# Node rows stored early, expert results added to them in DRAM by chained scatters

## The reference

```python
x = x + _L0_gnn_ref(_layernorm(x), src, dst, ...)      # six diffusion steps over 100 k edges
x = x + _L0_ffn_ref(_layernorm(x)[None], ...)[0]       # below

logits = einsum('bsd,de->bse', xn, Wr) + br
top_vals, top_idx = jax.lax.top_k(logits, 2)
w = jax.nn.softmax(top_vals, axis=-1)                  # two weights per node
for e in range(8):
    h = gelu(einsum(xn, W1[e]) + b1[e])
    y = y + (einsum(h, W2[e]) + b2[e]) * w_full[..., e, None]
```

## Time and profile before

| | us |
|---|---|
| median of 3 runs (range) | 1309.59 (1305.15 to 1309.78) |
| profiled execution, its own time | 1307.75 |
| its span, first to last instruction | 1305.6 |
| busy: PE, DVE, ACT, POOL | 1182.4, 726.9, 401.8, 201.5 |
| expert tiles: first scatter to last scatter | 1066.32 to 1275.06 |
| from the last scatter to the end of the span | 30.5 |

### The profile page before, as it was taken

One profiled execution on the slowest core, in us unless ns is written; L12 is line 12 of the kernel. 1 busy time (PEld: TensorE's weight loads), 2 busy tenths in 40 slices (PEclk: granted clock), 3 DMA queues, 4 the chain that ended last, 5 costly groups with the idle time before them and its releaser, 6 DMA issues.

```text
span 1305.6 us, 27942 instructions
## 1 busy us (share of the span) xinstructions
PE 1182.4 (91%) x7835; PEld 824.2 (63%) x7835; DVE 726.9 (56%) x1533; ACT 401.8 (31%) x785; POOL 201.5 (15%) x245
## 2 busy tenths in 40 slices
PE   5798999999999999999999999978998578898990
PEld 3586776665666666666666666645665367777770
DVE  7889999973444344432543444325556757644555
ACT  2675656550000000000221111101211154464553
POOL 2000000000111111111000000000111154455530
PEclk8998999999999999999999999998999789999995
DMA  6110011014443344323441233112333121122257
GB/s 158 45 50 25 25 37 31 28 37 121 100 99 83 61 109 103 88 55 77 130 129 40 85 108 104 57 29 60 114 112 111 52 86 58 62 71 72 75 151 208
DMA packets 76319, 106.02 MB, mean 81 GB/s; under 512 B 12929, under 2 KB 61880, under 8 KB 76108
## 3 DMA queue, kind: packets, MB, share of 16 engines
q1 hardware_dynamic: 62500, 72.44, 18.8%
q0 software_dynamic: 11376, 25.55, 8.7%
q10 hardware_dynamic: 2356, 6.93, 2.2%
HBM read 76.99 MB, written 37.49 MB: 88 GB/s over the span
## 4 chain that ended last, share of the span: by engine, by line
PE 70%; DVE 12%; issue 9%; DMA 3%; DVEq 2%; ACT 2%; POOL 1%; ACTq 1%; another core or an unknown queue 0%; SPq 0%; POOLq 0%
PE ps L1921 41%; PE ps L1899 7%; PE ps L2084 6%; PE ps L2070 6%; PE ps L1867 4%; DVE v_b L1165 3%; PE ps L1972 2%; POOL v_a L769 1%; PE ps L1835 1%; DMA h_ring<-h_dram 1%; PE ps L2056 1%; DMA adj<-y_dram 1%; PE ps L1846 1%; DVE adj L1072 1%; PE ps L2005 0%
## 5 line engine op out<-in xcount | busy, mean ns | idle before, releaser
L1921 PE MATMUL ps<-v_a,adj 125*125 125x512 f16 x1375 | 297.3, 379 | 0.0
L1921 PE MATMUL ps<-v_b,adj 125*125 125x512 f16 x1250 | 270.2, 379 | 1.8 <-DVE v_b L1190 1.8
L1921 PEld LDWEIGHTS ps<-v_a,adj 125*125 (+1 forms) x1375 | 187.6, 136 | 109.0
L1921 PEld LDWEIGHTS ps<-v_b,adj 125*125 x1250 | 170.6, 136 | 101.2 <-issue 2.2
L894 ACT ACTIVATE t_hi<-ps,cinv 125x256 f32<-125x256 f32 x125 | 59.2, 473 | 454.5 <-PE ps L1921 394.9
L1172 DVE SCALAR_TENSOR_TENSOR t_hi<-ps,cinv,t_hi 125x256 f32<-125x256 f32 x125 | 60.2, 482 | 234.5 <-ACT t_hi L894 234.5
L1165 DVE TENSOR_TENSOR v_b<-v_b 125x2560 f16<-125x2560 f16 x125 | 180.2, 1486 | 6.4 <-PE ps L1867 5.8
L1972 PE MATMUL ps<-v_b,adj 125*125 125x512 f16 x625 | 144.9, 392 | 7.7 <-POOL v_a L746 3.7
L869 ACT ACTIVATE adj<-ps 125x625 f32 (+1 forms) x125 | 112.2, 906 | 66.0 <-PE ps L1867 65.1
L2084 PE MATMUL ps<-adj,v_b 128*128 x672 | 112.8, 275 | 12.7 <-issue 6.1
L1972 PEld LDWEIGHTS ps<-v_b,adj 125*125 125x125 f16 (+1 forms) x625 | 86.4, 141 | 58.6 <-issue 5.5
(11 more groups left out here) (285 smaller groups left out, 977.8 us busy)
## 6 DMA issues: line engine op xcount, KB each, us to landing
h_ring<-h_dram SPq DMA_DIRECT2D x125, 125.0 KB
v_a<-L_ffn_W SPq DMA_DIRECT2D x32, 256.0 KB, 3.4
v_b<-L_ffn_W SPq DMA_DIRECT2D x32, 256.0 KB, 3.6
adj<-w_dram SPq DMA_DIRECT2D x16, 512.0 KB, 5.1
w_dram<-w_hi SPq DMA_DIRECT2D x32, 128.0 KB, 1.9
hx_dram<-h_dram POOLq DMA_DIRECT2D x25, 125.0 KB, 2.5
hx_dram<-x POOLq DMA_DIRECT2D x25, 125.0 KB, 3.3
hx_dram<-L_gnn_b_out POOLq DMA_DIRECT2D x25, 125.0 KB, 4.2
```

The lines of the kernel that those rows point to most:

```text
L1921: last = te.matmul(ps[0:NP, u, :], of_tile(adj[0:NP, 0:ADJ], i, u, a * NP, NP), source[:, a, :], start=(a == 0), stop=(a == T - 1))
```

## The change

The result of an expert tile is multiplied with its rows' weights on DVE and added by the scatter to the output in DRAM, which by then holds the node rows. A node may occur in two tiles, and an accumulating DMA reads, adds and writes, so each scatter waits until the one before has landed. The combining pass at the end is gone. The weights travel with the gathered rows: a row of `xs_dram` grows from 1024 to 1056 bytes, and they are computed earlier, in two parts. Cut to its core:

```diff
@@ SP, last step: x1 goes to out in groups of five tiles
+                    if u == 0 and (not isinstance(i, int) or i > 0):
+                        nodes_out(i - 1)
                     sp.dma_start(h_ring[0:NP, u % 2, :], ...)
+            def nodes_out(i):
+                for part in HALVES:
+                    sp.dma_start(out_v[part, group, :], x1[part, group, :]).then_inc(out_sem, 16)
+            def weights_out(t0, t1, done):
+                sp.wait_ge(S["wts_ok"], done)
+                sp.dma_start(xs_v[:, t0:t1, D:XS // 2], w_rows.bitcast(I32)[:, t0:t1, :]).then_inc(S["w_rows_in"], 16)
             last_step(sp, body)
+            weights_out(0, TA, 1)
+            sp.wait_ge(S["h_used"], LAST + T + 2)
+            nodes_out(NB - 1)
             for w in range(T - 6, T):
                 rows_out(w, w % WIN)
-            (wait for the low scatters, load y_dram's first half, store out in five groups)
+            weights_out(TA, T, 2)
+            sp.wait_ge(S["added"], 16 * FT)
             sp.wait_ge(out_sem, 32 * NB)
@@ POOL
+            pool.wait_ge(S["w_rows_in"], 16)
             pool.wait_ge(S["idx_ok"], 1)
             def gather(j):
                 if j >= FU:
                     pool.wait_ge(S["xg_T"], j - FU + 1)
+                    pool.wait_ge(S["hs_ok"], j - FU + 1)
             def scatter(j):
                 pool.wait_ge(S["y_ok"], j + 1)
-                g.indirect_dma_start(y_dram, ...).then_inc(y_out[r], 16)
+                need(pool, S["added"], 16 * j)
+                g.indirect_dma_start(out, ..., y_sb[r], None, bounds_check=N - 1, oob_is_err=False,
+                                     compute_op=ALU.add).then_inc(S["added"], 16)
+            pool.wait_ge(out_sem, 32 * NB)          # ahead of scatter 0
+            pool.wait_ge(S["w_rows_in"], 32)        # ahead of gather FA
@@ ACT: Exp at m == T - 2 and j == 10, no longer at j == FA + 4
+                    exponents(0, TA, 1)
                     for c in range(GA):
                         by_partition(planes_a, c, FA, c)
+                    a.activation(gb_max, gb_max, ACT.Sqrt)
-            (load y_dram's second half, multiply it with w_top2)
@@ DVE
 slots():         - min and max of a node's two places
 rows_of():       + is_first, is_second per row
 m == T - 3:      + margins(0, TA)         m == T - 2:  + row_weights(0, TA, 1)
 j == 9:            margins(TA, T)         j == 11:     + row_weights(TA, T, 2)
 j == 14, 18:     - low_tile(), low_count()     j == FA + 8: - row_weights()
             def hidden(j, b, e, part):
                 v.tensor_scalar(hh, h_g[r], sh[:, bass.ds(e, 1)], None, ALU.mult)
+                v.tensor_scalar(w_part[...], weights[:, 0:1], is_first[:, j:j + 1], None, ALU.mult)
                 v.drain()
+                v.scalar_tensor_tensor(w_slot[...], weights[:, 1:2], is_second[:, j:j + 1], w_part[...], ALU.mult, ALU.add)
                 v.scalar_tensor_tensor(hl, ...).then_inc(S["hs_ok"], 1)
             def result(j, b, e, part, alone):
-                need(dve, y_out[j % FR], 16 * (j // FR))
-                v.scalar_tensor_tensor(y_sb[u % FR], ...).then_inc(S["y_ok"], 1)
+                need(dve, S["added"], 16 * (j - FR + 1))
+                v.scalar_tensor_tensor(y, ...)
+                v.drain()
+                v.tensor_scalar(y, y, w_slot[:, j % FR:j % FR + 1], None, ALU.mult).then_inc(S["y_ok"], 1)
-            (the five combining groups on x1)
@@ PE: - the transpose for low_count
```

More of the change, by code:

```diff
@@ L327, in gnn_ffn @@
         ends_a = p20(NE + 1, F32)
-        low_top = p20(1, F32, NP)
-        low_end = p20(1, F32, 1)
-        tok_p, tok_c, tok_t, dest, empty, expert = (p21(FB, F32) for _ in range(6))
+        tok_p, tok_c, tok_t, empty, expert = (p21(FB, F32) for _ in range(5))
         le_tiles = p21(FB * NE, F32).rearrange("p (j e) -> p j e", e=NE)
@@ L334, in gnn_ffn @@
         assert FU == 8
-        x_g = [over(adj, ((9 if u < 4 else 14) * REG + XW) * 2 + u % 4 * 4 * D, 2 * D, F16) for u in range(FU)]
+        x_g = [over(adj, ((9 if u < 4 else 14) * REG + XW) * 2 + u % 4 * 2 * XS, XS, F16) for u in range(FU)]
         xT16 = [fc(2 * D, F16).rearrange("k (b s) -> k b s", b=2 * DK) for _ in range(XR)]
@@ L342, in gnn_ffn @@
         y_sb = [over(adj, at_y + r * D * 4, D, F32) for r in range(FR)]
[L344 to L347, removed]
+        assert XW + 4 * XS <= REG
         fe = taker(adj)
@@ L1020, in between @@
                     by_partition(planes_b, 4, FB, GA + 4)
[L1021 to L1023 removed]
+                if j == 10:
+                    exponents(TA, T, 2)
             def transposed(j):
@@ L1044, in _ @@
                 e = e_next
[L1046 to L1049, removed]
-                    act.dma_start(y_in[i][1][part], y_v[1, part, i * WIN:(i + 1) * WIN, :]).then_inc(yc_in[1][i], 16)
-            for i in range(NB):
-                act.wait_ge(yc_in[1][i], 32)
-                for t in range(WIN):
-                    n = i * WIN + t
-                    last = a.activation(y_in[i][1][:, t, :], y_in[i][1][:, t, :], ACT.Copy, scale=w_top2[:, n:n + 1])
-                last.then_inc(S["y2_ok"], 1)
         @block.vector
@@ L1523, in slots @@
                 n = TOP * tiles
-                v.tensor_tensor(s_all[:, 0:tiles], top[:, 0:tiles], top[:, tiles:n], ALU.min)
-                v.tensor_tensor(s_all[:, tiles:n], top[:, 0:tiles], top[:, tiles:n], ALU.max)
-                v.drain()
-                v.tensor_scalar(s_tile[:, 0:n], s_all[:, 0:n], 1.0 / 128, 1.0 / 256 - 0.5, ALU.mult, ALU.add)
+                v.tensor_scalar(s_tile[:, 0:n], top[:, 0:n], 1.0 / 128, 1.0 / 256 - 0.5, ALU.mult, ALU.add)
                 v.drain()
@@ L1564, in rows_of @@
             def rows_of(table, first, count):
-                p_, c_, t_, b_, no = (r[:, 0:count] for r in (tok_p, tok_c, tok_t, dest, empty))
+                p_, c_, t_, no = (r[:, 0:count] for r in (tok_p, tok_c, tok_t, empty))
+                second = is_second[:, first:first + count]
                 v.tensor_scalar(p_, table[:, 0:count], -1.0, 0.0, ALU.add, ALU.max)
@@ L1578, in rows_of @@
                 v.drain()
-                v.tensor_tensor(idx_s[:, first:first + count], p_, b_, ALU.add)
+                v.tensor_tensor(idx_s[:, first:first + count], p_, no, ALU.add)
                 v.drain().then_inc(S["idx_ok"], 1)
-            def low_tile():
-                v.tensor_tensor(swap, s_top[:, 0:T], s_all[:, 0:T], ALU.subtract)
-                v.tensor_reduce(low_top, s_tile[:, 0:T], AX.X, ALU.max)
-                v.drain().then_inc(S["low_in"], 1)
-                v.tensor_scalar(swap, swap, 0.0, None, ALU.is_gt)
@@ L1589, in low_count, with margins, row_weights @@
-            def low_count():
-                dve.wait_ge(S["low_ps"], 1)
-                v.tensor_reduce(low_end, ps[0:1, 7, 320:320 + NP], AX.X, ALU.max)
+            def margins(t0, t1):
+                v.tensor_tensor(m2[:, t0:t1], m2[:, t0:t1], m1[:, t0:t1], ALU.subtract)
+                v.drain().then_inc(S["ex_in"], 1)
+            def row_weights(t0, t1, done):
+                dve.wait_ge(S["ex_ok"], done)
+                v.tensor_scalar(den[:, t0:t1], ex2[:, t0:t1], 1.0, None, ALU.add)
```

110 lines of the change are left out of this document (38 added, 72 removed).

## The result

The changed kernel takes 1351.65 us (median of four runs, 1347.31 to 1354.08), the kernel before beside it 1308.57: 1.033 times as long, with a 95% interval of 1.0312 to 1.0354. The forecast was 1322 us in a range of 1300 to 1350; the sign was right, the time came out 30 us higher and just outside the range. The profiled execution took 1347.31 us over a span of 1345.5.

A forecast was written before the change was run, and what follows sets the result against it. PE was taken to set the second part's pace, 3.46 us a tile. Scatter 14 at 1139.4 + 41 x 4.30 + 4.02 for the last landing = 1319.7, plus 2.15 over the span: 1321.9, say 1322 us; range 1300 to 1350.

The forecast's parts named there:

- P: Second part: time from one chained scatter's start to the next, 1.28 + 2.17 + 0.57 + 0.28 = 4.30 us.
- The end: Behind the last scatter: 30.5 us of load, combining and stores go, only its own landing stays, 4.02 us.
- Scatter 14: Start of the second part's chain: moved from 1133.4 by 2 + 4 us to 1139.4, bounds 1135 to 1145.
- the store's wait: First gather waits for SP's 1875 weight pieces: gather 0 to 4 us late, PE about 1.2.
- The tables' stretch: Ahead of scatter 14, where the second part's tables are made: added DVE and ACT work costs 4 us.
- At nothing: Costs put at zero, among them ten stores to `out` under PE's last step; 3 us if that cover failed.
- The chain is hidden there: First part: tiles come every 4.79 us on average, over P, so chained scatters cost nothing.
- x's row: Accumulating x DMA in `sums`, 2.54 us behind its issue against the copy's 1.97: the add's price, 0.57 us.
- A nearly free add: Rival, second part: P at most 3.6, PE or DVE sets the pace, 1290 us, faster; chance 0.12.
- The bias rows' price: Rival, second part: a scatter costs what the accumulating bias rows do, P = 5.1, 1355 us; chance 0.15.
- No change at P = 4.0: Rival: POOL's issue does not grow, or part of the shift does not come, 1309 us; chance 0.2.
- Lost clock: Rival: PE drops to 1.2 GHz in the chain's gaps, 5.2 us a tile, 1360 us; chance 0.05.

The follow-up runs named there:

- the hand-off experiment: Changed kernel with the scatter's landing wait moved ahead of the wait for `y` and the bound put in a register once: 1323.18 us.

## Why the prediction was off, step by step

The mechanism and the sign were right: the scatters became a chain that sets the pace. The step that failed is the sum for P, 4.30 us where 4.71 was measured, and in it two terms taken from `sums`: 0.28 us from a landing to the next start (0.85 to 0.90 in its place) and 0.3 us for the dearer issue (0.6 in its place). The end, put at one landing, is the second step that failed. In order of time:

**Scatter 14** was forecast at 1139.4 and came at 1144.05, +4.7. The size of the store's wait was the wrong part: 7.2 us from issue to landing and 8.3 to the gather for 1875 pieces of 32 bytes, where 5.7 was taken from the earlier trace rows as the nearest row and 1.2 of it as what shows; the gather came 6.1 us late and 5 us of it showed. The tables' stretch was taken at 4 and measured at 5. "At nothing" did not hold in the last step: from POOL's first add of the last step to the last one ahead of the first gather, the kernels with the stores took 138.2 to 138.6 us, those without 135.4 to 136.0, about the 3 us that the prediction named for a failed cover. The kernel with two chains, which stores the node rows twice, took 148.8 us over the same stretch, so stores do cost time there; whether by their issues on SP or on the way is open. The add itself (125x256) also takes longer, 897 ns after and 812 before. That this trace's node tiles began 1.9 us earlier hid most of it.

"The chain is hidden there", of the first part, read an average. In the kernel before the first eight scatters were mostly 4.0 us apart, under even the forecast P; in the kernel after they were mostly 4.6 to 4.9 apart, and all but the first waited for a landing. Scatters 1 and 2 before, then 5 and 6 after:

```profile
1070.35 1.00 POOL L786 DMA_INDIRECT y_dram<-adj,v_a  x1 [1.74 <-DVE adj L1782]
1074.35 1.00 POOL L786 DMA_INDIRECT y_dram<-adj,v_a  x1 [1.71 <-DVE adj L1782]
```
```profile
1095.52 1.66 POOL L791 DMA_INDIRECT out<-adj,v_a  x1 [1.94 <-DMA out<-adj,v_a]
...
1100.28 1.59 POOL L791 DMA_INDIRECT out<-adj,v_a  x1 [1.81 <-DMA out<-adj,v_a]
```

It cost little at scatter 14 all the same, because that one stands behind the gathers of tiles 22 to 24, which wait for the second tables: counted from the same add it came after 103.6 us in the kernel after, 103.8 without the add and 101.7 with two chains, so at most 2 of the 5 us are the chain's.

**The link P** was forecast at 4.30 and measured at 4.71, which over 41 tiles is 17 of the 25 us between the forecast's 1321.9 and the profiled 1347.31. Term by term:

| us | forecast | measured | from |
|---|---|---|---|
| issue | 0.98 + 0.30 | 1.59 | the timeline above |
| issue's end to landing, plain | 2.17 | 1.43 | the kernel without the add |
| what the add puts there | 0.57 | 0.7 | the same |
| landing to next start | 0.28 | 0.85 to 0.90 | the chain above |

The four measured terms add up to 4.6. The mean is 4.71, since five links ended on a late DVE and some landings beside gathers took up to 4.3 us, against three empty links of 3.57. Three of the four terms are off, in both directions. The plain landing came from one row, the last scatter, an empty tile whose rows all go to spare rows; with real rows it is 0.7 us less. The growth of the issue was taken from DMAs with 125 rows named by no index and is twice theirs. The term that failed worst is the last: 0.28 us holds where the awaited landing is the last thing ahead of the DMA, and the prediction read it off `sums` without asking what would stand between wait and scatter in the new program. That the landing was 0.7 us too long and the hand-off 0.6 too short is luck, and brought the forecast nearer than its terms were; the 0.3 of the issue and 0.1 of the add are left.

What stood of the reasoning: the add is priced by x's row, 0.57 against 0.7, not by the bias rows' 1.39. By the Trainium skill ("DMA: Bandwidth & Descriptors", "Why a DMA increments its semaphore by 16 and not by 1"), 125 rows lie on 5 engines and 128 on 16; the measured 0.7 lies near x's price, as that would have it. But no run shows on how many engines a DMA lay, and the same section names an exception on trn2 by which some direct copies from POOL lie on all 16 whatever their rows. The skill's 2.3 us for a POOL DMA of 128 KB (same page, "Anatomy of one DMA — SWDGE (gpsimd) path") has no term for the add. Here the plain scatter's 2.42 us from start to landing agree with it; the prediction had matched it with the 2.17 us behind the issue of an empty tile. The adding one landed mostly 3.7 to 4.1 us after its start.

**The end** was forecast at 4.0 us, one landing, and took 8.2. The landing is there (2.71 us for an empty tile), but POOL's drain of 6.5 us runs behind the last issue and is the last thing to end. In the kernel before it could be read (1274.7 to 1285.2) and was under a tail of 30.5 us: a cover that the change took away, and that the prediction did not look under.

4.7 + 16.9 + 4.2 = 25.8 us, against the 25.4 between 1321.9 and 1347.31; the other 0.4 is that the time was 1.8 us over the span and not 2.15. The remaining 4.3 us to the median are spread: the profiled run was the fastest of four, and it alone would have been inside the range.

**The rivals.** A nearly free add: the kernel without the add shows the rival's pace (3.56 us a tile against its 3.55), but the add is not free. The bias rows' price: right in its total (1355 us, P = 5.1, near the measured median), wrong in its reason, since P was 4.71 and the add costs 0.7 at the landing; start and end made up the rest. No change at P = 4.0: neither of its conditions came, the issue grew by 0.6 us and the shift was 10.7 and not 6; and the hand-off experiment came to P = 4.09 and still to 1323 us, since start and end were dearer than forecast. Lost clock: 0.93 over the second part against 0.98, PE busy 1.5 us more; not it. Of the marks to look for, scatters released by a DMA, DVE waiting before its `y` and gaps in PE were right, and spacing, the end and scatter 14 were each too low.

## What to carry to other kernels

When transfers are put in a row, the price is their latency, and it has four parts: issue, landing, what the operation adds to either, and the way from a released wait to the next start; count each from rows of the same kind of transfer in the same place, and look at what stands between the last wait and the instruction. Ask of any chain whether all of its links are needed: here only tiles of different experts can hit the same row, and chaining those alone brought back 58 to 60 us (with the weights' store in halves, whose own part is 2.4 at most). When a tail is removed, read what ran under it, closing drains too.

## What the runs showed of the hardware that was not expected

- An accumulating indirect DMA from POOL keeps POOL for 1.59 us, a plain one for 0.98; and one whose rows are all out of bounds still takes 1.55 us to issue and 2.71 from its start to its landing.
- A second instruction between a released wait and an indirect DMA costs some 0.55 us: 0.77 to 0.90 us from landing to start with a MOVE or an earlier wait between, 0.28 without.
- POOL's program ends with 6.5 us of drain behind the issue of its last adding scatter, 9.2 behind that of a plain one.
- 1875 pieces of 32 bytes from SP took 7.2 us from issue to landing; split by partitions (112 and 13) 4.1.
- The same program ran 3.46 us a tile in one job and 3.07 in another, with 11.9 us of waits on PE without a releaser in the first.
